# Decoder scores of a pair in eight 32x64 tiles and four banks, both transposes in the odd unit, and a ring of three banks

## The reference

```python
def mha(xq, xkv, W, B, mask):
    q, k, v = proj(xq, W[0], B[0]), proj(xkv, W[1], B[1]), proj(xkv, W[2], B[2])
    score = jnp.einsum('bhqd,bhkd->bhqk', q, k) / math.sqrt(DH)
    if mask is not None:
        score = jnp.where(mask[:, None] == 0, -10000.0, score)
    attn = jax.nn.softmax(score, axis=-1)
    out = jnp.einsum('bhqk,bhkd->bhqd', attn, v)
    return out.transpose(0, 2, 1, 3).reshape(bsz, -1, D) @ W[3] + B[3]

def step(x, p):
    x = layer_norm(mha(x, x, saw, sab, mask) + x, lg[0], lb[0])
    x = layer_norm(mha(x, enc, caw, cab, None) + x, lg[1], lb[1])
    x = layer_norm(jax.nn.relu(x @ W1 + B1) @ W2 + B2 + x, lg[2], lb[2])
```

## Time and profile before

| what | value |
|---|---|
| median of 3 runs | 4544.5 us (4528.99 to 4550.94) |
| profiled execution | 4549.62 us, span 4547.8 us |
| PE busy | 3983.5 us (88%), granted clock 0.934 in the mean |
| DVE busy | 2617.2 us (58%) |
| ACT busy | 1875.0 us (41%) |
| scores L2284, busy on PE | 211.3 us, 3072 records |

### The profile page before, as it was taken

The page is one execution under the profiler, slowest core; times in us unless marked ns, Lnnn a source line. Parts: engine busy times, 40 slices in busy tenths (PEclk is TensorE's granted clock), DMA queues, the critical chain, the costliest instruction groups (busy, mean ns, idle before and its releaser), DMA issues. The chain is left out here.

```text
span 4547.8 us, 103588 instructions
## 1 busy us (share of the span) xinstructions
PE 3983.5 (88%) x43122; PEld 2985.0 (66%) x43122; DVE 2617.2 (58%) x5484; ACT 1875.0 (41%) x5200; POOL 300.4 (7%) x560
## 2 busy tenths in 40 slices
PE   7988996999999999999999997779588787789867
PEld 6766884677777777777777775568355577566635
DVE  3435114777777777777777774611467555255535
ACT  1221221444444445444444443222366444156523
POOL 0000101000000000000000000110211000000000
PEclk9998997999999999999999998889799888888878
DMA  4110484001101101111111100057444200010000
GB/s 149 60 58 3 164 299 134 29 27 43 57 27 49 51 30 46 52 42 34 51 42 34 59 22 10 2 215 282 162 143 157 89 0 0 28 35 20 11 1 12
DMA packets 116916, 310.46 MB, mean 68 GB/s; under 512 B 29352, under 2 KB 75625, under 8 KB 92017
## 3 DMA queue, kind: packets, MB, share of 16 engines
q1 hardware_dynamic: 113392, 295.61, 19.0%
q0 software_dynamic: 3072, 8.39, 0.5%
HBM read 289.01 MB, written 14.94 MB: 67 GB/s over the span
## 5 line engine op out<-in xcount | busy, mean ns | idle before, releaser
L2524 ACT COPY layers_pT<-banks 128x512 f32<-128x512 f32 x384 | 227.3, 592 | 606.9 <-PE banks L2292 606.2
L2223 PE MATMUL banks<-weights_a,ctx_tiles 128*128 128x256 f32 x1536 | 363.6, 380 | 0.0
L2216 PE MATMUL banks<-ctx_tiles,weights_a 128*128 128x512 f32 x768 | 363.2, 595 | 0.0
L2517 ACT ACTIVATE layers_probs<-banks,layers_negmax 128x256 f32<-128x256 f32 x768 | 354.2, 480 | 13.5 <-DVE layers_negmax L2382 6.5
L2223 PEld LDWEIGHTS banks<-weights_a,ctx_tiles 128*128 128x128 f32 x1536 | 285.2, 191 | 76.3 <-issue 46.5
L2360 DVE TENSOR_TENSOR layers_V<-banks,rows_a 128x512 f32<-128x512 f32 x192 | 130.8, 681 | 215.5 <-PE banks L2223 215.5
L2292 PE MATMUL banks<-const,layers_probs 128*128 128x128 f32 x1536 | 244.1, 281 | 3.4 <-ACT layers_pT L2524 2.8
L2292 PEld LDWEIGHTS banks<-const,layers_probs 128*128 128x128 f32 x1536 | 171.2, 141 | 107.1 <-issue 97.1
L2381 DVE TENSOR_REDUCE layers_negmax<-banks 128x4 f32<-128x1024 f32 x192 | 233.7, 1217 | 2.8 <-PE banks L2284 2.6
L2484 ACT ACTIVATE layers_KT<-banks,layers_less_last 128x256 f32<-128x256 f32 x384 | 162.1, 480 | 157.1 <-PE banks L2216 157.1
L2284 PE MATMUL banks<-layers_KT,layers_qblk 32*64 32x256 f32 x3072 | 211.3, 389 | 0.0
(11 more groups left out here) (702 smaller groups left out, 8443.0 us busy)
## 6 DMA issues: line engine op xcount, KB each, us to landing
ctx_tiles<-in_ctx SPq DMA_DIRECT2D x65, 1028.0 KB, 5.0
weights_a<-in_L_w SPq DMA_DIRECT2D x44, 1024.0 KB, 6.9
l2x_B<-positions SPq DMA_DIRECT2D x32, 1280.0 KB, 5.9
weights_b<-in_L_w SPq DMA_DIRECT2D x32, 1024.0 KB
weights_c<-in_L_w SPq DMA_DIRECT2D x16, 1024.0 KB
weights_b<-in_L_xattn_w SPq DMA_DIRECT2D x12, 1024.0 KB, 6.5
l0x_key_rows<-in_ctx_rows SPq DMA_DIRECT2D x32, 256.0 KB, 2.6
ctx_tiles<-in_ctx_keys SPq DMA_DIRECT2D x32, 256.0 KB, 2.8
```

The source lines that it names most:

```text
L2216: last = mm(o.rearrange("p (j k) -> p j k", j=2), ca_wk[:, c, m * P:(m + 1) * P], keys, start=c == 0, stop=c == DC - 1)
L2223: last = mm(o[:, b * D:(b + 1) * D], E.ctx[:, tile % 2, c, first:first + P], ca_wv[:, c], start=c == 0, stop=c == DC - 1)
L2517: a(probs[:, cc, i, t], ps[:, t, i % 2 * KW:(i % 2 + 1) * KW], ACT.Exp, bias=negmax[:, cc, t, i:i + 1], accum_out=totals[:, cc, t, i:i + 1 ...
L2524: nc.scalar.copy(pT[:, k % 4].rearrange("p t c x -> p (t c x)"), ps[:, TURN]).then_inc(s["copied"], 1)
```

## The change

The eight score products of a pair get one tile each: product (r, a), with r the 32 rows of its heads and a the unit of the pair, writes to bank 2a + r//2 and to the partition half (r + a) % 2. Before, the half was r % 2 for both units, and both units shared banks 0 and 1. The scores take the lower halves of banks 0 to 3. Their upper halves take the transposes, of both units of a pair together, in the odd unit, at the place in the job list that `TURN_AT` names. ACT copies both there. `values` and `shares` follow the changed halves; `shares` is eight products over half of the columns. PV moves to bank 4 and the ring of jobs to banks 5 to 7. V(3) moves from unit 5 to unit 6, DVE does `self_shares` behind the maxima of unit 4 and not at the unit's end, and ACT takes D2 after the exponentials of unit 6.

```diff
@@ -2044,3 +2044,4 @@
     U = DC * GB
-    TURN, PV, RING, RB = 2, 3, 4, 4
+    PV, RING, RB = 4, 5, 3
+    TURN_AT = {1: 2, 3: 1, 5: 1, 7: 1}
 
@@ -2058,4 +2059,4 @@
         [("D0", None, "act"), k_job(3), ("S2", None, "dve")],
-        [("D1", 0, "act"), v_job(3), ("S6", None, "dve")],
-        [("D2", 1, "act"), ("X", None, "act")],
+        [("D1", 0, "act"), ("S6", None, "dve")],
+        [("D2", 1, "act"), v_job(3), ("X", None, "act")],
         [("S7", None, "dve"), ("D3", None, "dve")],
@@ -2279,7 +2280,8 @@
                         need_evacuated(pe, pos, "K", (DC - 1, 1))
-                    need(pe, "exp_done", 2 * k)
-                    for a in range(2):
-                        for r in (0, 2, 1, 3):
-                            rows, half = slice(32 * r, 32 * (r + 1)), slice(64 * (r % 2), 64 * (r % 2 + 1))
-                            last = mm(ps[half, r // 2, a * KW:(a + 1) * KW], qblk[rows, tile % 2, cc, j + a], KT[rows, tile % 2, cc, (j + a) * KW:(j + a + 1) * KW], start=True, stop=True)
+                    need(pe, "copied", k)
+                    for r in range(4):
+                        for a in range(2):
+                            side = (r + a) % 2
+                            rows, half = slice(32 * r, 32 * (r + 1)), slice(64 * side, 64 * (side + 1))
+                            last = mm(ps[half, 2 * a + r // 2, 0:KW], qblk[rows, tile % 2, cc, j + a], KT[rows, tile % 2, cc, (j + a) * KW:(j + a + 1) * KW], start=True, stop=True)
                     last.then_inc(s["scores_done"], 1)
@@ -2287,8 +2289,8 @@
                 def transposes(k, pos, cc, j):
-                    need(pe, "exp_done", 2 * (k + 1))
-                    need(pe, "copied", k)
-                    for t in range(2):
-                        for c in range(KC):
-                            last = tr(ps[:, TURN, (KC * t + c) * P:(KC * t + c + 1) * P], probs[:, cc, j, t, c * P:(c + 1) * P], E.c("ident"))
-                    last.then_inc(s["transposed"], 1)
+                    pe.wait_ge(s["exp_done"], 2 * (k + 2))
+                    for a in range(2):
+                        for t in range(2):
+                            for c in range(KC):
+                                last = tr(ps[:, 2 * a + t, KW + c * P:KW + (c + 1) * P], probs[:, cc, j + a, t, c * P:(c + 1) * P], E.c("ident"))
+                        last.then_inc(s["transposed"], 1)
 
@@ -2303,3 +2305,4 @@
                         for i in range(4):
-                            last = mm(ps[32 * i:32 * (i + 1), PV, j * 64:(j + 1) * 64], V[:, pos % 2, KC * j + c, cc * P + 32 * i:cc * P + 32 * (i + 1)], pT[:, k % 4, i // 2, c, 64 * (i % 2):64 * (i % 2 + 1)], start=c == 0, stop=c == KC - 1)
+                            side = (i + j) % 2
+                            last = mm(ps[32 * i:32 * (i + 1), PV, j * 64:(j + 1) * 64], V[:, pos % 2, KC * j + c, cc * P + 32 * i:cc * P + 32 * (i + 1)], pT[:, k % 4, i // 2, c, 64 * side:64 * (side + 1)], start=c == 0, stop=c == KC - 1)
                     last.then_inc(s["pv_done"], 1)
@@ -2307,4 +2310,7 @@
                         pe.wait_ge(s["spread_ready"], k // GB + 1)
-                        for i in range(4):
-                            last = mm(ps[32 * i:32 * (i + 1), PV, D:2 * D], E.c("headcol")[:, 32 * (i % 2):32 * (i % 2 + 1)], spread[:, i // 2].rearrange("p s j q -> p (s j q)"), start=True, stop=True)
+                        for a in range(2):
+                            for i in range(4):
+                                side = (i + a) % 2
+                                last = mm(ps[32 * i:32 * (i + 1), PV, D:2 * D].rearrange("p (s i a q) -> p s i a q", s=2, a=2, q=LQ)[:, :, :, a], E.c("headcol")[:, 32 * side:32 * (side + 1)],
+                                          spread[:, i // 2].rearrange("p s (i a) q -> p s i a q", a=2)[:, :, :, a], start=True, stop=True)
                         last.then_inc(s["shares_done"], 1)
@@ -2314,6 +2320,9 @@
                         scores(*ca_unit(it))
-                    if ca_unit(it - 2):
-                        transposes(*ca_unit(it - 2))
-                    for a in jobs_in(it):
+                    turn_at = TURN_AT.get(it % U)
+                    for i, a in enumerate(jobs_in(it)):
+                        if i == turn_at and ca_unit(it - 1):
+                            transposes(*ca_unit(it - 1))
                         job(*a)
+                    if turn_at is not None and len(jobs_in(it)) <= turn_at and ca_unit(it - 1):
+                        transposes(*ca_unit(it - 1))
                     for back in (3, 2):
@@ -2380,3 +2389,3 @@
                     peak = negmax[:, cc, :, j:j + 2]
-                    link(v.tensor_reduce(peak, ps[:, 0:2].rearrange("p t (a x) -> p t a x", a=2), AX.X, ALU.max, negate=True))
+                    link(v.tensor_reduce(peak.rearrange("p t a -> p a t"), ps[:, 0:4, 0:KW].rearrange("p (a t) x -> p a t x", a=2), AX.X, ALU.max, negate=True))
                     v.tensor_scalar(peak, peak, 0.0, None, ALU.min).then_inc(s["max_ready"], 1)
@@ -2437,2 +2446,4 @@
                         maxima(*ca_unit(it))
+                    if u == 4 and steps[step]["sa"] is not None:
+                        self_shares(steps[step]["sa"])
                     for a in jobs_in(it):
@@ -2451,4 +2462,2 @@
                         self_shift(steps[step]["sa"])
-                    if u == 4 and steps[step]["sa"] is not None:
-                        self_shares(steps[step]["sa"])
                     for a in unfinished:
@@ -2516,3 +2525,3 @@
                         for t in range(2):
-                            a(probs[:, cc, i, t], ps[:, t, i % 2 * KW:(i % 2 + 1) * KW], ACT.Exp, bias=negmax[:, cc, t, i:i + 1], accum_out=totals[:, cc, t, i:i + 1]).then_inc(s["exp_done"], 1)
+                            a(probs[:, cc, i, t], ps[:, i % 2 * 2 + t, 0:KW], ACT.Exp, bias=negmax[:, cc, t, i:i + 1], accum_out=totals[:, cc, t, i:i + 1]).then_inc(s["exp_done"], 1)
                     if j == GB - 2:
@@ -2523,3 +2532,3 @@
                     need(act, "pv_done", k - 3)
-                    nc.scalar.copy(pT[:, k % 4].rearrange("p t c x -> p (t c x)"), ps[:, TURN]).then_inc(s["copied"], 1)
+                    nc.scalar.copy(pT[:, k % 4].rearrange("p t c x -> p t (c x)"), ps[:, k % 2 * 2:k % 2 * 2 + 2, KW:2 * KW]).then_inc(s["copied"], 1)
 
@@ -2528,6 +2537,4 @@
                     early = 0
-                    if ca_unit(it - 2):
-                        copy_transposed(*ca_unit(it - 2))
                     if it % 2 == 0 and ca_unit(it):
-                        while jobs_in(it)[early:early + 1] and early < 1 + (jobs_in(it)[0][3] == "XK"):
+                        while u != 6 and jobs_in(it)[early:early + 1] and early < 1 + (jobs_in(it)[0][3] == "XK"):
                             take(*jobs_in(it)[early])
@@ -2535,4 +2542,12 @@
                         exponentials(*ca_unit(it))
-                    for b in jobs_in(it)[early:]:
-                        take(*b)
+                    turn_at = TURN_AT.get(u)
+                    for i, b in enumerate(jobs_in(it)):
+                        if i == turn_at and ca_unit(it - 1):
+                            for back in (1, 0):
+                                copy_transposed(*ca_unit(it - back))
+                        if i >= early:
+                            take(*b)
+                    if turn_at is not None and len(jobs_in(it)) <= turn_at and ca_unit(it - 1):
+                        for back in (1, 0):
+                            copy_transposed(*ca_unit(it - back))
                     if steps[step]["sa"] is not None and u == 3:
```

## The result

The changed kernel is slower: median 4585.66 us (4581.96 to 4587.9, 4 runs) against 4542.33 us (median of 4 runs of the kernel before), so 43.3 us more. The ratio is 1.0097, with a 95% interval of 1.0071 to 1.0123. The forecast was 4578 us and slower. Its profiled execution has a span of 4582.5 us, 34.7 more than before.

A forecast was written before the change was run, and what follows sets the result against it. PE was taken to bound the decoder. Plain steps +1.26-0.42-0.31+0.28=+0.81 us, layer-opening steps +0.22; over 40 and 6 steps +34 us, 4583 profiled, so 4578 as median; own range 4560 to 4600, 8-in-10 range 4495 to 4630.

The forecast's parts named there:

- Scores: A pair's score products on PE: one turn instead of two, about 0.60 us for 1.02, gaining 0.42 per pair.
- The rival that they would go four at a time: Eight score tiles still work four at a time, scores stay at 1.02 us; 4617 us, chance 0.05.
- Unit 0 to unit 2: Job n, a state transpose, waits 1.65 us for S1q's emptying in the ring of three; stretch costs 1.26 us.
- Rival (b): Only the wait before job n, a state transpose, is absent or short, the others come; 4506 us, chance 0.17.
- Unit 2 to unit 4: Stretch between these units' scores: no wait, length 10.29 us against 10.71, gain 0.42.
- Unit 4 to unit 6: Stretch with waits of 0.54 us before the transposes and 0.85 before S6; length 9.46, gain 0.31.
- Unit 6 to unit 0: Stretch to the next step's scores, waits of 0.48 us before transposes and 0.40 before D3; length 11.00, cost 0.28.
- the steps that open a layer: Each layer's first decoder step, 6 counted: +1.26-0.42-0.31-0.31=+0.22 us each.
- X hides the first wait and nearly all of the second: Unit 6 to unit 0 in a layer's first step: X, 0.82 us, covers waits; length 11.00, gain 0.31.
- Rival (e), the clock: Decoder clock falls to half rate for 3.4 us, losing 1.7, in half the steps; 4616 us, chance 0.08.
- a granted clock below 1.00 inside the decoder: One of the signs named beforehand that would show the forecast wrong: PE's clock below full 2.4 GHz there.
- Rival (c): The step's five waits together some 0.8 us smaller than worked out; no change, 4545 us, chance 0.20.

The follow-up runs named there:

- e3: The changed kernel with the scores back in four different tiles, still in four banks; 4624.45 us, ratio 1.0182 to the kernel before.
- e12: The changed kernel with three VectorE orders moved (feed-forward norm, self_shift, own_heads) and the scores back in four tiles; 4505.55 us, ratio 0.9917 to the kernel before.
- e1: The changed kernel with the feed-forward's closing norm on VectorE moved behind the emptying of S1q; 4531.38 us, ratio 0.9976 to the kernel before.
- e2: The kernel before with only its ring of job banks cut from four to three; 4630.02 us, ratio 1.0202 to the kernel before.
- e5: The changed kernel with VectorE's self_shift moved ahead of V2's emptying in unit 3; 4541.63 us, ratio 0.9976 to the kernel before.
- e8: The changed kernel with own_heads of the first half of the heads moved behind unit 6's maxima; 4560.25 us, ratio 1.0017 to the kernel before.
- e4: The changed kernel with ScalarE emptying D2 ahead of unit 6's exponentials; 4568.74 us, ratio 1.0063 to the kernel before.
- e7: The changed kernel with V3 moved back from unit 6 to unit 5; 4679.82 us, ratio 1.0278 to the kernel before.

## Why the prediction was right

The direction, the size and the places were right. Step by step:

**Scores.** 0.405 us less per pair, 0.42 forecast; e3 and e12 show that this is the tiles' doing. The rival that they would go four at a time is out.

**Unit 0 to unit 2.** 11.54 us, 11.71 forecast. V0's end (4.34) and DVE's 5.76 us were exact. The size that was off is the release: I took 0.26 us from S6's wait, and n began 0.06 after the row of S1q's emptying ended. The step that I had read was not a regular one either. In the kernel before, S6 came 0.15 us behind the stream transpose (L2427) in 43 of its 48 waits and 0.26 behind it in the other five; the next step has the regular one, after a stream transpose that ended at 1776.05:

```profile
1776.20 1.10 PE L2255 MATMUL banks<-layers_sa_pT,layers_sa_v 128*32 128x64 f32 x64 [1.04 <-DVE layers_sa_pT L2427]
```

e1 and e2 show the cause from both sides: without the ring of three no wait in the kernel before, with it 1.9 us; with S1q emptied sooner no wait in the changed kernel. Rival (b) is out in the changed kernel, and e1 is what it would have been: 4531 us, 4506 forecast. Its plain step is 0.77 us below before's, near the 0.84 of the rival; what keeps the time up is the step that opens a layer, 0.36 above before's, and 11 us of irregular idle time.

**Unit 2 to unit 4.** 10.40, 10.29 forecast. No wait, as said. The 0.11 is the first job behind the scores: q's eight records take 1.00 us from start to start where they take 0.89 behind other transposes.

**Unit 4 to unit 6.** 9.17, 9.46 forecast. Transposes at 5.72 (5.80), S6 at 7.26 (7.52). Again the release was sized too large, 0.26 us where it was 0.10; the other 0.1 is DVE's chain, which ended at 7.15 and not 7.26. e5 shows that the chain on DVE is the bound: moved by 0.9 us, both waits go.

**Unit 6 to unit 0.** 10.91, 11.00 forecast, with transposes at 5.48 (5.53) and D3 at 6.70 (6.80). ScalarE's release measured 0.05 us, where I took 0.15. e8 shows own_heads as the head of that chain.

**Where it was wrong: the steps that open a layer.** I gave them 43.20 us, +0.22; they take 44.60, +1.62. The step that failed is "X hides the first wait and nearly all of the second". X is a job and takes a place in the ring. So S7, behind it, takes the bank of D2, and ACT empties D2 late, behind the exponentials. The row of S7 (L2261) behind X (L2233):

```profile
1783.53 0.97 PE L2233 MATMUL banks<-last_keys,weights_a 128*128 128x32 f32 x8
1785.90 1.13 PE L2261 MATMUL banks<-weights_c,layers_sa_attnT 128*128 128x256 f32 x4 [1.40 <-ACT layers_hid L2516]
```

I had followed the ring through the plain step only. e4 empties D2 early and these 1.6 us go. The plain step was sized too large instead: 42.46 against 42.02. I had also measured it from 41.65, a step ahead of one that opens a layer and with the longer release before S6, where the regular one was 41.54; so +0.81 stands against +0.48. Over 40 and 6 steps that is 32+1 forecast and 19+10 measured, so the two errors nearly cancel in the sum; part of the good agreement is luck. The remaining 6 of the 34.7 us between the profiled executions are irregular. Some are idle times at scattered places for which no releaser is shown, three of 1.4 to 1.8 us in the changed kernel. Some are the clock: between the decoder's first and last steps it fell twice, at 2253.1 us behind an idle time of 1.25 us inside a score group, and at 2126.8 behind such a wait of S7:

```profile
2125.00:2127.00 2.00, 1.22 (x6) 1.07 (x7) 0.05 (x1) 1.09 (x5) 0.00 (x0) 0.96 0.85 341
2127.00:2130.40 3.40, 3.40 (x14) 3.02 (x13) 2.25 (x6) 1.17 (x2) 0.79 (x2) 0.52 0.19 77
```

The medians of the runs are 43.3 us apart and not 34.7, mostly because the profiled execution of the kernel before (4549.62) was 7 us above its median. The forecast had 34. The interval of the ratio, 32 to 56 us, holds it, but some 8 us more are in no row of this account.

**Rival (e), the clock**, did not come as it needed, in half of the steps: the wait before n was 1.25 us, and the clock was 1.00 over the middle 600 us. The prediction named a granted clock below 1.00 inside the decoder as a sign of being wrong, and two falls are there; they cost a few us of the 43. A wait as long as the 1.65 us of this rival is in e2, 1.71 us before n in 44 steps, with 3 falls; 1.95 us in e7 gave 33. So the kind of loss is real, and a wait of this rival's length brings it rarely. Falls inside the decoder could have been read from the trace of the kernel before as well: 0.50 from 816.9 to 820.3 us, behind a wait of 2.83 us of S6, nearer to this case than the rows of l1a.

**Rival (c)**, smaller waits, holds in part: from start to start PE lost 1.42, 0.46, 0.67, 0.37 and 0.35 us at the five places, together 3.3 of the 3.9 worked out. It was not enough for no change.

## What to carry to other kernels

When an edit takes a buffer from a ring, write down for every job which one it now follows, in every kind of step, and look up when that one is emptied and what stands ahead of it on the emptying engine. A saving on the busiest engine counts only in the stretches that it sets itself; the others show as short waits, and each has a chain whose order can often be changed for nothing. Here three moved orders on VectorE turned a loss of 1.0% into a gain of 2.4%; two moves in the old layout alone gave 1.3%, so compare a new layout with the old one in its own best order. And read a wait's release over many steps: the one step that the prediction read had the rarer value.

## What the runs showed of the hardware

Eight 32x64 tiles of fp32, with two of them on the same 32 rows and with two row bands in one bank at different partition halves, run together at full rate: 0.618 us for a group of eight products over 256 columns, against 1.023 for two turns of four. One turn more costs 0.425 us (e3's 1.043 less 0.618), what a full product of 256 columns takes (0.43). ScalarE's and VectorE's reads of the score banks cost nothing extra; VectorE's maxima took 1213 ns in the mean over four banks and 1217 over two, ScalarE's exponentials 473 and 480. The time from the end of a releaser's row to PE's start is not one number: in the changed kernel 0.06 us before n (VectorE) and 0.05 before the transposes (ScalarE), 0.10 before S6, and in the kernel before 0.15 before S6 in 43 waits and 0.26 in five. What sets it stays open.

The granted clock fell for 3.4 us at a time, behind idle times of very different length: 0.69 us inside a score group of e3 (at 1460.0 us), 1.25 us inside one of the changed kernel (at 2253.1), 1.40 us before S7 there (at 2126.8), 1.71 us before n in 3 of the 44 waits of e2, and 1.95 us in most steps of e7. Idle times of the same lengths also passed without a fall, so their length alone does not decide it. What else does, no run here shows.
